# Counts of repeated edges made by VectorE and written by plain scatters, in groups of eight behind each chunk's sixteen gathers

## The chip, the cores and the metric

The kernel runs on one core of one Trainium2 chip. The metric is device time in microseconds (us) of that core; lower is better. The engines are named as in the profile: PE (TensorE), DVE (VectorE), ACT (ScalarE), POOL (GpSimd), SP (SyncE).

## What is computed

Four graph layers run one after another over the same 6250 nodes of 128 features and the same 106250 edges, which are sorted by receiver. Each layer is added to its input and normalised:

```python
edge_index = jnp.stack([src, dst])
x = _layernorm(x + _L0_gnn_ref(x, edge_index, ...))                  # attention, both directions
x = _layernorm(x + _L1_gnn_ref(x, ..., src, dst, edge_type_4))       # two attention layers, 4 relations
x = _layernorm(x + _L2_gnn_ref(x, edge_index, ...))                  # graph convolution
x = _layernorm(x + _L3_gnn_ref(x, edge_index, edge_weight1, ...))    # sum over edges, then a two-layer network
```

The part that the change touches is a matrix that the last two layers use. Their sums over edges are of this kind:

```python
msgs = h[src] * norm[:, None]
agg = jax.ops.segment_sum(msgs, dst, num_segments=n) + b
```

The kernel computes them as a dense product with a matrix `adj` of edge counts: the entry for receiver r and sender s is how many edges run between them, 0 for most, 1 for most of the rest, 2 or more where an edge is repeated.

## The kernel before

The edges lie as 128 partitions of `EC` = 832 columns, in the order of the receiver. The stages run one after the other, with a barrier between them: sorting and counting (`place_edges` twice, called plc1 and plc0; plc0 also makes the tables by edge, in steps called `table_part`, one per group of 8 columns), two sweeps of the first layer, a turn layer t0, the attention sweep of the second layer's first half (below: first sweep), turn layer t1, the second attention sweep (second sweep), turn layer t2, and the dense layers.

An attention sweep goes over the 832 columns in `NCK` = 52 chunks of `CK` = 16. For each chunk POOL issues 16 indirect gathers of one column each (128 rows of 256 words out of the node table, tile `l_swp_G`, L1465), into a ring of `GR` = 4 chunks. DVE makes the 16 query rows (`query`, L1580), multiplies and reduces them (`multiply`, `reduce`), and does the running maximum, the weighting and the long scan of the softmax (L1605 to L1645); ACT turns values, exponentiates and makes the result rows; SP loads queries and stores rows. POOL may start the gathers of chunk c when DVE's `weigh` of chunk c - 4 has told `used`. DVE handles chunk c's front part while it makes the queries of chunk c + 1, and waits in `multiply` for the gathers of chunk c + 1. When the last row is stored, POOL gathers the rows of first segments (`l_swp_FR`), DVE and PE merge the ends of partitions, and POOL scatters them back.

`adj` has 2-byte entries and is cleared early. It is filled by 832 indirect DMAs, one per column of edges, each of which adds the constant 1 into 128 cells (`CELL` holds the numbers of the cells). Two adds into one cell must not be in flight together, so `put_cell` (L1410) has POOL wait, before each add, until the one before has landed:

```python
pool.wait_ge(g.landed, 16 * g.put)
pool.indirect_dma_start(out=g.cells, ..., in_=g.ONE[:, 0:1], in_offset=None, compute_op=ALU.add)
```

These adds stand in POOL's program between other work: 49 in turn layer t0 (one behind each scatter of queries, `put_query`, L1807), then in the first sweep one behind every second gather (`EVERY` = 2, so 8 per chunk), with 8 and 3 more at its end, 49 in t1, and the rest in the second sweep, where the last of them starts at 7761.3 us and the last chunks have gathers alone. In the turn layers PE, DVE and ACT make a query row for each of 49 groups of nodes; `t_qr` is a ring of four of them, emptied by `put_query`.

## Time and profile before

| | |
|---|---|
| median of 3 runs | 9291.03 us (9284.9 to 9291.43) |
| the profiled execution | 9288.31 us, span 9286.2 us |
| busy over the span | POOL 62%, DVE 54%, ACT 31%, PE 30% |
| first sweep, first gather to end of last | 3849.7 to 5899.1 us |
| second sweep, the same | 6244.3 to 8035.5 us |
| turn layers | t0 3504 to 3850 us, t1 5949 to 6244 us, t2 8078 to 8254 us |

The profiled execution is 2.7 us under the median and within the range of the runs. Busy shares are means over stages with different limits; the stage is what counts. Indirect DMAs are listed on POOL by the time in which POOL writes their descriptors; the transfer itself follows.

### The profile page before, as it was taken

What the parts mean: (1) busy time and instruction counts of PE and PEld (TensorE: products, weight loads), DVE (VectorE), ACT (ScalarE), POOL (GpSimd) and SP (SyncE); (2) the same over time, 40 slices, a digit from 0 to 9 for tenths busy, and PEclk for the clock granted to TensorE, in tenths of its full rate; (3) what the DMA queues carried; (4) which work ended last, traced back from release to release, by engine and by line L of the source; (5) the groups of instructions that cost most, each with busy time, mean ns of one, the idle gap of its engine ahead of it and who ended that gap; (6) DMA issues with size and microseconds to landing.
All of it is one profiled execution on the core that took longest, in us unless ns stands there. A gap on an engine that the chain in (4) does not pass through costs nothing. (4 is left out here: it accounts for less than half of the span.)

```text
span 9286.2 us, 65164 instructions
## 1 busy us (share of the span) xinstructions
PE 2819.9 (30%) x19883; PEld 2216.5 (24%) x19883; DVE 4982.0 (54%) x8546; ACT 2921.4 (31%) x3159; POOL 5776.8 (62%) x5419
## 2 busy tenths in 40 slices
PE   5666635555100005400000000270000000059997
PEld 5666525555100005300000000160000000034443
DVE  7555547766699996444444444434444446740212
ACT  6333313333366662222222222232222223410001
POOL 2777777777777767677777777657777777610000
PEclk8555555555555557755555555585555555569998
DMA  5655224444466655444444434453444445546653
GB/s 140 212 197 191 82 72 143 130 135 133 152 217 217 219 198 155 134 109 111 111 110 111 110 103 111 112 156 98 110 111 111 111 111 159 182 72 192 196 189 115
DMA packets 576000, 1306.03 MB, mean 141 GB/s; under 512 B 249724, under 2 KB 344654, under 8 KB 521766
## 3 DMA queue, kind: packets, MB, share of 16 engines
q1 hardware_dynamic: 252742, 889.07, 28.3%
q0 software_dynamic: 292960, 358.27, 16.7%
q10 hardware_dynamic: 29952, 54.54, 2.4%
q8 instruction: 161, 2.64, 0.1%
q14 instruction: 185, 1.52, 0.1%
HBM read 782.92 MB, written 518.52 MB: 140 GB/s over the span
## 5 line engine op out<-in xcount | busy, mean ns | idle before, releaser
L1465 POOL DMA_INDIRECT l_swp_G<-table,KVI x1664 | 1605.2, 965 | 512.5 <-issue 327.1
L1410 POOL DMA_INDIRECT adj<-ONE,CELL x832 | 1344.2, 1616 | 728.0 <-DMA adj<-ONE,CELL 486.7
L1586 DVE TENSOR_TENSOR l_swp_PROD<-l_swp_G,l_swp_QS 128x1024 f32<-128x1024 f32 x208 | 253.9, 1221 | 2005.5 <-DMA l_swp_G<-table,KVI 2005.4
L1691 PE MATMUL l_swp_AW<-l_swp_ET,ones 128*128 128x512 f32 x4 | 4.2, 1141 | 3932.3 <-DVE l_swp_ET L1669 3932.3
L1110 POOL DMA_INDIRECT arrived<-plc_QS,plc_idx x832 | 814.1, 979 | 253.6 <-issue 245.4
L1110 POOL DMA_INDIRECT slots<-REC,plc_idx x832 | 796.9, 958 | 273.4 <-issue 252.8
L1522 ACT ACTIVATE l_swp_VT<-l_swp_G 128x2048 f32<-128x2048 f32 x104 | 385.8, 3710 | 1826.6 <-issue 1692.4
L1195 POOL DMA_INDIRECT l_G<-table,OTHI x832 | 786.2, 945 | 256.1 <-issue 252.9
L1691 PEld LDWEIGHTS l_swp_AW<-l_swp_ET,ones 128*128 128x128 f32 x4 | 1.0, 312 | 3932.6 <-DVE l_swp_ET L1669 3932.6
L949 PE MATMUL plc_pr<-plc_seen,plc_otf 128*128 128x49 f32 x3328 | 861.6, 414 | 12.8 <-DVE plc_seen L698 12.8
L949 PEld LDWEIGHTS plc_pr<-plc_seen,plc_otf 128*128 128x128 f32 x3328 | 846.8, 326 | 32.4 <-issue 32.1
L1580 DVE SCALAR_TENSOR_TENSOR l_swp_QS<-l_swp_QS,KEEP,l_swp_QX 128x128 f32<-128x128 f32 x1664 | 586.6, 353 | 44.3 <-DMA l_swp_QX<-queries 6.7
L1332 DVE TENSOR_TENSOR_SCAN l_X<-l_AW,l_X 128x2244 f32<-128x2244 f32 x104 | 502.5, 4831 | 3.6
L1639 DVE TENSOR_TENSOR_SCAN l_swp_X<-l_swp_AW,l_swp_X 128x2244 f32<-128x2244 f32 x104 | 501.0, 4818 | 0.1
L1063 ACT ACTIVATE plc_otb<-plc_otf 128x1024 bf16<-128x1024 f32 x208 | 219.9, 1057 | 778.7 <-PE plc_pe_q L938 775.1
L759 DVE SCALAR_TENSOR_TENSOR plc_QS<-plc_QS,KEEP,plc_QX 128x136 f32<-128x136 f32 x831 | 288.4, 347 | 316.2 <-DMA arrived<-plc_QS,plc_idx 173.1
L951 PEld LDWEIGHTS plc_pr<-plc_ohi,plc_bm 128*128 128x128 bf16 x1664 | 445.2, 268 | 0.0
L2448 PE MATMUL dn_acc<-dn_AR,HP 128*128 128x512 f16 (+1 forms) x1950 | 424.4, 375 | 33.8 <-DMA dn_AR<-adj 30.9
L2448 PE MATMUL dn_acc<-dn_AR,dn_HP 128*128 128x512 f16 (+1 forms) x1950 | 419.8, 372 | 4.8 <-ACT dn_HP L2657 2.0
L1263 ACT ACTIVATE l_ROW<-l_X 128x2112 f32<-128x2112 f32 x104 | 407.5, 3918 | 2.2 <-DVE l_X L1332 2.2
L1543 ACT ACTIVATE l_swp_ROW<-l_swp_X 128x2112 f32<-128x2112 f32 x104 | 407.5, 3918 | 0.0
L951 PE MATMUL plc_pr<-plc_ohi,plc_bm 128*128 128x49 bf16 x1664 | 394.3, 237 | 0.0
(502 smaller groups left out, 8294.6 us busy)
## 6 DMA issues: line engine op xcount, KB each, us to landing
sums<-l_ROW SPq DMA_DIRECT2D x104, 1088.0 KB, 4.7
l_swp_QX<-queries SPq DMA_DIRECT2D x104, 1088.0 KB, 7.8
dn_AR<-adj SPq DMA_DIRECT2D x100, 832.0 KB, 4.6
adj<-plc_zrow SPq DMA_DIRECT2D x100, 800.0 KB
dn_AR<-adj SPq DMA_DIRECT2D x100, 768.0 KB, 4.3
queries<-plc_zrow SPq DMA_DIRECT2D x55, 1088.0 KB
sums<-l_swp_ROW SPq DMA_DIRECT2D x52, 1096.0 KB, 5.5
plc_QX<-queries SPq DMA_DIRECT2D x104, 544.0 KB, 4.4
```

Source lines behind the costliest of these rows:

```text
L949: pe.matmul(pr[:, b, j * NB:(j + 1) * NB], otf[:, c % FB, j, :], seen[:, b, :, j], start=True, stop=False)
L951: last = pe.matmul(pr[:, b, j * NB:(j + 1) * NB], bm[:, b, j, :], column(ohi[:, c % HB, :, :, :], j), start=False, stop=True)
L1110: pool.indirect_dma_start(out=slots, out_offset=bass.IndirectOffsetOnAxis(ap=idx[:, c % IB, j:j + 1], axis=0), in_=g.REC[:, c * CH + j, :] ...
L1195: pool.indirect_dma_start(out=G[:, p % GR, j, :], out_offset=None, in_=table, in_offset=bass.IndirectOffsetOnAxis(ap=g.OTHI[:, x:x + 1], a ...
L1263: act.activation(ROW[:, c % 2, :, 0:D + H], X[:, c % 2, :, :, 1:CK + 1].rearrange("p h d c -> p c (h d)"), ACT.Copy).then_inc(rowed, 1)
L1332: v.tensor_tensor_scan(X[:, b, :, :, :].rearrange("p h d c -> p (h d c)"), AF[:, :, :, :].rearrange("p h d c -> p (h d c)"), X[:, b, :, :, ...
L1410: pool.indirect_dma_start(out=g.cells, out_offset=bass.IndirectOffsetOnAxis(ap=g.CELL[:, g.put:g.put + 1], axis=0), in_=g.ONE[:, 0:1], in_ ...
L1465: pool.indirect_dma_start(out=G[:, c % GR, j, :], out_offset=None, in_=table, in_offset=bass.IndirectOffsetOnAxis(ap=index[:, c * CK + j:c ...
L1543: act.activation(ROW[:, c % 2, :, 0:D + H], X[:, c % 2, :, :, 1:CK + 1].rearrange("p h d c -> p c (h d)"), ACT.Copy).then_inc(rowed, 1)
L1580: v.scalar_tensor_tensor(out=QS[:, j, :], in0=QS[:, j - 1 if j else QH - 1, :], scalar=g.KEEP[:, n:n + 1], in1=QX[:, c % QB, x, 0:D], op0= ...
L1639: v.tensor_tensor_scan(X[:, b, :, :, :].rearrange("p h d c -> p (h d c)"), AF[:, :, :, :].rearrange("p h d c -> p (h d c)"), X[:, b, :, :, ...
L2448: last = pe.matmul(acc[m][:, 0:z], HP[:, j, part, :], AR[:, i % RING_A, (q - first) * P:(q - first) * P + z], start=(j == 0 and part == 0) ...
```

## The change

The adds become plain scatters. In plc0, `table_part` gets eight more steps (i from 11 to 18): a key per edge (`KEY`: receiver times 8192 plus sender, as f32) and a mark (`AGAIN`) on an edge whose key stands earlier in its group of 8 columns. In the two attention sweeps DVE takes 8 columns of edges per chunk. For each of the eight, `later` compares the key with all keys to the right of it in its partition and counts the equal ones with the instruction's accumulator. Then `cells` looks with `max_index` for an equal key to the left, adds 1 to the counts (`VAL`), and points the cell of every edge that is not the first of its kind to a spare cell. So the first edge of a kind writes the whole count, and nothing is added in memory. The eight scatters of a chunk stand behind its 16 gathers, `BEHIND` = 5 chunks after DVE has handled them; they wait for `celled`, never for a landing. The turn layer t0 has no scatters into `adj` any more, t1 has 16, each sweep has 16 + 8 at its end, and t2 has 16 behind its fetches, before the dense layers read `adj`.

```diff
-EVERY = 2
+BEHIND = 5
...
+                elif i == 11:
+                    link(v.tensor_tensor_scan(t[:, :], F[:, :], F[:, :], 0.0, ALU.add, ALU.max))
+                    link(v.scalar_tensor_tensor(out=g.KEY[:, :], in0=t[:, :], scalar=float(1 << SHIFT), in1=g.OTHI[:, :],
+                                                op0=ALU.mult, op1=ALU.add))
+                    link(v.memset(g.AGAIN[:, :, :], 0.0))
+                    v.tensor_scalar(g.SPARE[:, :], g.minus[:, :], float(-(1 << SHIFT)), float((NB + 1) * P), ALU.mult, ALU.add)
+                elif i < 19:
+                    d = i - 11
+                    key = g.KEY[:, :].rearrange("p (q i) -> p q i", i=8)
+                    same = t[:, 0:EC // 8 * (8 - d)].rearrange("p (q i) -> p q i", i=8 - d)
+                    link(v.tensor_tensor(same, key[:, :, d:8], key[:, :, 0:8 - d], ALU.is_equal))
+                    link(v.tensor_tensor(g.AGAIN[:, :, d:8], g.AGAIN[:, :, d:8], same, ALU.max))
...
-def put_cell(pool, passed, g):
-
-
-    if g.put < EC:
-        if g.put:
-            pool.wait_ge(g.landed, 16 * g.put)
+def put_cell(pool, passed, g, upto):
+
+
+    if g.put < upto * 8:
+        if g.put % 8 == 0:
+            pool.wait_ge(g.celled, g.put // 8 + 1)
             passed()
         pool.indirect_dma_start(out=g.cells, out_offset=bass.IndirectOffsetOnAxis(ap=g.CELL[:, g.put:g.put + 1], axis=0),
-                                in_=g.ONE[:, 0:1], in_offset=None, compute_op=ALU.add).then_inc(g.landed, 16)
+                                in_=g.VAL[:, g.put:g.put + 1], in_offset=None).then_inc(g.landed, 16)
         g.put += 1
...
-                    if j % EVERY == EVERY - 1:
-                        put_cell(pool, passed, g)
-            for _ in range(8):
-                put_cell(pool, passed, g)
+                if c >= BEHIND:
+                    for _ in range(8):
+                        put_cell(pool, passed, g, (part + 1) * NCK)
+            for _ in range(16):
+                put_cell(pool, passed, g, (part + 1) * NCK)
...
-            for _ in range(3):
-                put_cell(pool, passed, g)
+            for _ in range(8):
+                put_cell(pool, passed, g, (part + 1) * NCK)
...
+            def later(c, i):
+                q = part * NCK + c
+                x = q * 8 + i
+                if i >= 2:
+                    v.wait_ge(told, pick.n + i - 1)
+                if x == EC - 1:
+                    v.memset(RPT[:, i:i + 1], 0.0).then_inc(told, 1)
+                else:
+                    v.tensor_scalar(EQ[:, x % 2, 0:EC - 1 - x], g.KEY[:, x + 1:EC], g.KEY[:, x:x + 1], 0.0, ALU.is_equal, ALU.add,
+                                    accum_out=RPT[:, i:i + 1]).then_inc(told, 1)
+
+            def cells(c):
+                q = part * NCK + c
+                at = slice(q * 8, q * 8 + 8)
+                v.max_index(FIND[:, :], g.KEY[:, at], g.KEY[:, 0:q * 8 + 8]).then_inc(told, 1)
+                pick.n += 9
+                v.wait_ge(told, pick.n)
+                v.tensor_scalar(g.VAL[:, at], RPT[:, :], 1.0, None, ALU.add)
+                pick(v.scalar_tensor_tensor(out=DROP[:, 0, :], in0=FIND[:, :], scalar=float(-q * 8), in1=g.iota[:, 0:8],
+                                            op0=ALU.add, op1=ALU.not_equal))
+                v.tensor_tensor(DROP[:, 1, :], DROP[:, 0, :], g.AGAIN[:, q, :], ALU.max)
+                pick(v.tensor_scalar(AWAY[:, :], g.iota[:, 0:8], g.SPARE[:, 0:1], float(q * 8), ALU.add, ALU.add))
+                pick(v.copy_predicated(g.CELL[:, at], DROP[:, 1, :], AWAY[:, :]))
+                v.sem_inc(g.celled, 1)
...
+                    if c >= 0 and x % 2 == 1:
+                        later(c, x // 2)
...
+                if c >= 0:
+                    cells(c)
```

On POOL, in the first sweep, one chunk reads before like this (`l_swp_G` are the gathers, `adj` the adds), eight times over:

```order
L1465 DMA l_swp_G<-table,KVI 128x256 x2
L1410 DMA adj<-ONE,CELL 52428800x1
L1465 DMA l_swp_G<-table,KVI 128x256 x2
L1410 DMA adj<-ONE,CELL 52428800x1
L1465 DMA l_swp_G<-table,KVI 128x256 x2
```

And the same engine at the start of that sweep after the change:

```order
L1484 DMA l_swp_G<-table,KVI 128x256 x96
L1422 DMA adj<-VAL,CELL 52428800x1 x8
L1484 DMA l_swp_G<-table,KVI 128x256 x16
L1422 DMA adj<-VAL,CELL 52428800x1 x8
L1484 DMA l_swp_G<-table,KVI 128x256 x16
```

The first six chunks of gathers have nothing between them, and from then on 8 scatters stand behind each 16 gathers.

On DVE, in the first sweep, the middle of a chunk after the change (chunk 1; `l_swp_QS` are the query rows, `l_swp_EQ,l_swp_RPT<-KEY` are `later`'s compares):

```order
L1651 TENSOR_TENSOR l_swp_X<-l_swp_VT,l_swp_AW 128x4x32x16
L1676 TENSOR_SCALAR l_swp_EQ,l_swp_RPT<-KEY 128x821
L1601 SCALAR_TENSOR_TENSOR l_swp_QS<-l_swp_QS,KEEP,l_swp_QX 128x128
L1660 SCALAR_TENSOR_TENSOR l_swp_X<-l_swp_AW,l_swp_X 128x2244
L1601 SCALAR_TENSOR_TENSOR l_swp_QS<-l_swp_QS,KEEP,l_swp_QX 128x128
L1666 COPY l_swp_X<-l_swp_X 128x132
L1676 TENSOR_SCALAR l_swp_EQ,l_swp_RPT<-KEY 128x820
L1607 TENSOR_TENSOR l_swp_PROD<-l_swp_G,l_swp_QS 128x1024
```

Two of the chunk's eight compares are seen here, inside the chain that ends in `used` and in the next chunk's products; before the change the same rows stand without them. At the chunk's end come the six instructions of `cells`:

```order
L1611 TENSOR_REDUCE l_swp_LB<-l_swp_PROD 128x8x4 x2
L1682 MAX_INDEX l_swp_FIND<-KEY 128x8
L1685 TENSOR_SCALAR VAL<-l_swp_RPT 128x8
L1686 SCALAR_TENSOR_TENSOR l_swp_DROP<-l_swp_FIND,iota 128x8
L1688 TENSOR_TENSOR l_swp_DROP<-l_swp_DROP,AGAIN 128x8
L1689 TENSOR_SCALAR l_swp_AWAY<-iota,SPARE 128x8
L1690 COPY_PREDICATED CELL<-l_swp_DROP,l_swp_AWAY 128x8
```

The compare's length shrinks by one with each column, from 831 elements in the first chunk of the first sweep to 416 at its end, and from 415 to 0 in the second sweep; the length that `max_index` looks through grows by 8 a chunk, from 8 to 832.

## Rows read from the trace of the kernel before

**Rows 1.** The page, busy time, share and instructions of each engine
```profile
PE 2819.9 (30%) x19883; PEld 2216.5 (24%) x19883; DVE 4982.0 (54%) x8546; ACT 2921.4 (31%) x3159; POOL 5776.8 (62%) x5419
```

**Rows 2.** Busy us of each engine in two stretches, the two sweeps
```profile
3849.70:5899.10 2049.40, 0.00 (x0) 0.00 (x0) 898.83 (x1445) 520.66 (x357) 1474.81 (x1247) 0.50 0.41 109
6244.30:8035.50 1791.20, 0.00 (x0) 0.00 (x0) 893.50 (x1441) 522.01 (x406) 1296.37 (x1139) 0.50 0.44 124
```

**Rows 3.** POOL's groups by line, first sweep (busy, mean | idle before, releaser)
```profile
L1465 POOL DMA_INDIRECT l_swp_G<-table,KVI x832 | 805.3, 968 | 256.3 <-issue 151.0 <-DMA adj<-ONE,CELL 105.4
L1410 POOL DMA_INDIRECT adj<-ONE,CELL x415 | 669.5, 1613 | 321.4 <-DMA adj<-ONE,CELL 199.9 <-issue 121.5
```

**Rows 4.** POOL's groups by line, second sweep
```profile
L1465 POOL DMA_INDIRECT l_swp_G<-table,KVI x832 | 799.9, 961 | 256.1 <-issue 176.1 <-DMA adj<-ONE,CELL 77.1 <-POOLq L93 2.9
L1410 POOL DMA_INDIRECT adj<-ONE,CELL x307 | 496.5, 1617 | 241.6 <-DMA adj<-ONE,CELL 154.2 <-issue 87.4
```

**Rows 5.** POOL's timeline, first sweep (start, us, operation, idle before)
```profile
4311.40 1.61 POOL L1410 DMA_INDIRECT adj<-ONE,CELL  x1 [4.18 <-DMA adj<-ONE,CELL]
```

**Rows 6.** Adds into adj, issue to landing
```profile
DMA to landing us min/median/max: 2.9/3.1/9.1
```

**Rows 7.** POOL's groups by line where no adds are left
```profile
L1465 POOL DMA_INDIRECT l_swp_G<-table,KVI x161 | 152.2, 946 | 49.0 <-issue 49.0
```

**Rows 8.** POOL's groups by line, whole span
```profile
L1110 POOL DMA_INDIRECT arrived<-plc_QS,plc_idx x832 | 814.1, 979 | 253.6 <-issue 245.4 <-DVE plc_idx L721 7.9 <-DMA arrived<-plc_QS,plc_idx 0.3
L1827 POOL DMA_INDIRECT adj<-ONE,ODD x1 | 1.0, 984 | 0.3 <-issue 0.3
```

**Rows 9.** DVE's timeline, second sweep, no adds left
```profile
7917.26 1.22 DVE L1586 TENSOR_TENSOR l_swp_PROD<-l_swp_G,l_swp_QS 128x1024 f32<-128x1024 f32 x1 [2.28 <-DMA l_swp_G<-table,KVI]
7937.27 1.22 DVE L1586 TENSOR_TENSOR l_swp_PROD<-l_swp_G,l_swp_QS 128x1024 f32<-128x1024 f32 x1 [2.26 <-DMA l_swp_G<-table,KVI]
```

**Rows 10.** DVE's groups by form, whole span
```profile
L844 DVE TENSOR_SCALAR plc_tab_t<-plc_tab_F 128x832 f32<-128x832 f32 x1 | 0.6, 595 | 0.0
L438 DVE TENSOR_REDUCE plc_tab_small<-plc_tab_t 128x1 f32<-128x832 f32 x2 | 2.0, 1020 | 0.1
L851 DVE TENSOR_TENSOR_SCAN shared<-plc_tab_t,plc_tab_rec 128x832 f32<-128x832 f32 x4 | 7.6, 1894 | 0.0
L721 DVE TENSOR_SCALAR plc_idx<-plc_pos 128x8 uint32<-128x8 f32 x208 | 40.8, 196 | 447.7 <-DMA slots<-REC,plc_idx 445.3
```

**Rows 11.** Timeline of a turn layer, DVE and POOL side by side
```profile
3547.50 1.08 DVE L1988 TENSOR_TENSOR HH<-HH,t_par 128x896 f32<-128x896 f32 x1
3547.59 1.80 POOL L1792 DMA_INDIRECT t_NV<-sums,LASTI  x1 [0.30 <-issue]
```

**Rows 12.** POOL's timeline, ends of the two sweeps
```profile
5945.74 0.99 POOL L1481 DMA_INDIRECT sums<-l_swp_FR,BACKI  x1 [0.30 <-issue]
...
8065.02 0.95 POOL L1475 DMA_INDIRECT l_swp_FR<-sums,FIRSTI  x1 [29.52 <-DMA sums<-l_swp_ROW]
8074.64 0.98 POOL L1481 DMA_INDIRECT sums<-l_swp_FR,BACKI  x1 [8.67 <-DVE l_swp_FR L1686]
```

**Rows 13.** POOL's timeline, first and last of the query scatters in two turn layers
```profile
3577.99 0.98 POOL L1807 DMA_INDIRECT queries<-t_qr,STARTI  x1 [0.30 <-issue]
...
3841.89 0.99 POOL L1841 DMA_INDIRECT t_first<-queries,SEGI  x1 [0.30 <-issue]
...
6013.38 1.00 POOL L1807 DMA_INDIRECT queries<-t_qr,STARTI  x1 [0.30 <-issue]
...
6236.93 0.99 POOL L1841 DMA_INDIRECT t_first<-queries,SEGI  x1 [0.31 <-issue]
```

**Rows 14.** ACT's timeline, two query rows in succession
```profile
6104.37 0.27 ACT L2162 ACTIVATE t_qr<-t_pq 128x128 f32<-128x128 f32 x1
...
6108.42 0.27 ACT L2162 ACTIVATE t_qr<-t_pq 128x128 f32<-128x128 f32 x1
```

**Rows 15.** Waits in 1410 to 1560 us: total us, times, longest
```profile
DVE plc_QS L759 <- DMA arrived<-plc_QS,plc_idx: 29.1, 11, 4.2
```

More of the change, by code:

```diff
@@ L916, in _ @@
                     reached(n)
-                    if 0 <= c - 1 < 11:
+                    if 0 <= c - 1 < 19:
                         table_part(c - 1)
@@ L1400, in _ @@
                 o.then_inc(added, 1)
-def put_cell(pool, passed, g):
-    if g.put < EC:
-        if g.put:
-            pool.wait_ge(g.landed, 16 * g.put)
+def put_cell(pool, passed, g, upto):
+    if g.put < upto * 8:
+        if g.put % 8 == 0:
+            pool.wait_ge(g.celled, g.put // 8 + 1)
             passed()
         pool.indirect_dma_start(out=g.cells, out_offset=bass.IndirectOffsetOnAxis(ap=g.CELL[:, g.put:g.put + 1], axis=0),
-                                in_=g.ONE[:, 0:1], in_offset=None, compute_op=ALU.add).then_inc(g.landed, 16)
+                                in_=g.VAL[:, g.put:g.put + 1], in_offset=None).then_inc(g.landed, 16)
         g.put += 1
 def attention_sweep(nc, g, k, table, width, index, voff, array, out, weights, tag):
+    part = 1 if weights else 0
     ro = RO + 1 if weights else RO
@@ L1430, in attention_sweep @@
         weighed = s.sem("weighed")
+        told = s.sem("told")
+        RPT = s.sb("RPT", [P, 8])
+        EQ = s.sb("EQ", [P, 2, EC], BF16)
+        FIND = s.sb("FIND", [P, 8], U32)
+        DROP = s.sb("DROP", [P, 2, 8], U32)
+        AWAY = s.sb("AWAY", [P, 8], U32)
         init = s.sem("init")
@@ L1561, in _ @@
             link = Chain(v, chain)
+            pick = Chain(v, told)
             v.memset(FL[:, :, :, 0:1], -BIG)
@@ L1816, in _ @@
                         put_query(n - AHEAD * GT + 1)
-                        put_cell(pool, passed, g)
                 for n in range(NB - AHEAD * GT + 1, NB):
                     put_query(n)
-                    put_cell(pool, passed, g)
             else:
@@ L1823, in _ @@
                     fetch(n)
-                    if gcn and n % 3 == 2:
-                        put_cell(pool, passed, g)
                 if gcn:
@@ L1829, in _ @@
                     for _ in range(EC):
-                        put_cell(pool, passed, g)
+                        put_cell(pool, passed, g, 2 * NCK)
                     pool.wait_ge(lone, 16)
@@ L1835, in _ @@
                         put_query(n)
-                        put_cell(pool, passed, g)
+                        put_cell(pool, passed, g, NCK)
             if not gcn:
@@ L2782, in gnn_kernel @@
         g.ONE = sb("ONE", [P, 1], F16)
+        g.KEY = sb("KEY", [P, EC])
+        g.VAL = sb("VAL", [P, EC], F16)
+        g.AGAIN = sb("AGAIN", [P, EC // 8, 8], BF16)
+        g.SPARE = sb("SPARE", [P, 1])
+        g.celled = nc.alloc_semaphore("celled", num=max(nc.free_semaphores))
         g.landed = nc.alloc_semaphore("landed", num=max(nc.free_semaphores))
```

## The prediction

> **What bounds the kernel now.** I read the busy shares first: POOL 62%, DVE 54% [rows 1]. No engine is near full, so the stages have to be looked at one by one. In the two attention sweeps (2049.4 and 1791.2 us, 41% of the span together) DVE is busy 899 and 894 us, ACT 521 and 522, PE not at all, POOL 1475 and 1296 [rows 2]. The groups of POOL by line close the account: in the first sweep the gathers take 805.3 busy + 256.3 idle = 1061.6 us and the adds 669.5 + 321.4 = 990.9, together 2052.5 of 2049.4 [rows 3]; in the second 1056.0 + 738.1 = 1794.1 of 1791.2 [rows 4]. So POOL's program in order is the length of a sweep, and half of it is the adds: 2.39 us for each (990.9 / 415), of which 1.61 is the writing of descriptors and the rest waits. The reader is to see one such wait in the timeline: POOL stands 4.18 us before an add, released by the landing of the one before [rows 5]; adds land 2.9 to 9.1 us after their issue, 3.1 in the median [rows 6].
>
> **The sweeps, POOL.** Once the adds have run out, a gather costs (152.2 + 49.0) / 161 = 1.250 us [rows 7], so 832 cost 1040 us. The price of a plain scatter: the nearest row in kind is the one into `adj` of a single column with 2-byte data, 0.984 + 0.3 us; the nearest in number are the 832 scatters of plc0, issued eight in a row, (814.1 + 253.6) / 832 = 1.283 us [rows 8]. They agree, and I take 1.283. Bounds: 1.250, as a gather; above, no row of these reaches the add's 1.92. From first to last gather of a sweep stand 46 groups of eight (behind chunks 5 to 50): 368 x 1.283 = 472 us. A sweep is then 1512 us: 2049.4 - 1512 = 538 less in the first, 1791.2 - 1512 = 279 less in the second. The second gains less since its last 14 chunks have no adds now.
>
> **The sweeps, DVE.** This holds only while DVE needs less than POOL's 16 x 1.250 + 8 x 1.283 = 30.3 us for a chunk. Without adds the same DVE work repeats every 7937.27 - 7917.26 = 20.01 us with 2.26 idle: 17.75 us [rows 9]. New are eight compares and `cells`. The trace has no compare with an accumulator and no `max_index`. From below: a plain TENSOR_SCALAR over 832 f32 takes 0.595 us; from above: a scan, which carries a value from element to element, 1.894; between them a reduction, which like the compare reads one f32 tensor and gives one value, 1.020; one over 8 elements takes 0.196 [rows 10]. I take the reduction as nearest in kind: 0.19 + 0.0010 n us. The mean length in the first sweep is 623: 0.81 x 8 = 6.5 us; `cells` is one look through 212 elements in the mean, 0.4, and five small ones at 0.2, 1.4 together. DVE: 17.75 + 6.5 + 1.4 = 25.7 us a chunk, 27.2 in the first chunks. In the second sweep the mean length is 207: 17.75 + 3.2 + 1.8 = 22.8. Both lie under 30.3, so DVE's addition costs nothing; the cover is 4.6 us a chunk in the first sweep, and beyond it each us costs 52. The first five chunks are gathers alone, 20.0 us each, and DVE at 27.2 falls behind. POOL is held only if `weigh` of chunk c - 4 is late: for chunk 5, wanted at 100 us, it comes at about 25 + 2 x 27.2 + 8 = 87 us. From there POOL is the slower one. `celled` is told some four chunks before its scatters.
>
> **The shared resource.** In a turn layer an indirect DMA on POOL takes 1.80 us instead of 0.95 while DVE runs a TENSOR_TENSOR on two SBUF tensors of 896 elements [rows 11]. The sweep's long DVE instructions do not show this: gathers there stay at 0.946 us [rows 7]. Of the new ones three a chunk read two SBUF tensors or more, over 8 elements, 0.2 us each. If each met POOL, 3 x 0.2 x 104 = 62 us; I take 10. The Trainium skill, page "SBUF — State Buffer", section "Who interferes with whom", says that `tensor_scalar` in a two-port mode locks GpSimd out of a shared port pair, but not in the form that writes out its accumulator. By that rule the eight compares cost POOL nothing; if the exception did not hold here, the sum would be that of the second rival. No row of before shows the accumulating form.
>
> **Ends of the sweeps.** From the end of the last gather to the end of the scatter back it is 5946.7 - 5899.1 = 47.6 us in the first and 8075.6 - 8035.5 = 40.1 in the second, where no adds stand and the rows are ready 29.5 us after the last gather [rows 2, 12]. After: 24 scatters are 30.8 us, then the gather of first rows 1.25, eight scatters 10.3 (DVE's merge of 8.7 lies under them), 1.3 for the scatter back: 43.6 in each. DVE's last chunk has up to 4 us more, mostly under ACT's rows. Sum 4 less, 3.5 more: 0.
>
> **Turn layers.** t0 from its first query scatter to the gather that follows the last takes 263.9 us, t1 223.6, each with 49 adds among 49 queries [rows 13]. Without adds the other engines set the pace: two successive query rows are 4.05 us apart where nothing is waited for [rows 14]. Four rows are ready at the start, so the floor is 45 x 4.05 + 5 = 187 us. t1 keeps 16 scatters, 1.3 + 1.3 us with the query beside them, under 4.05. Other waits (normalisation once per seven groups, transfers) stay: between floor and now I take 4.8 us a row in t0, which has more of them, and 4.25 in t1: 220 and 195 us, 44 and 28 less. Ends: floor in both (77 and 37 less), or nothing.
>
> **What I cost at nothing.** plc0's new steps: the first is one scan (1.9), one pass (1.1), a memset and a small one, about 3.6 us; the other seven are two passes over 416 elements in the mean, about 1.2 us. In that stretch DVE waits 29.1 us of 150 for landings of POOL's scatters alone, about 2 us in a chunk of 10 [rows 15]; uncovered it would be 12 us. The 16 scatters in t2 end at about 8170 us by today's clock, the layer at 8254.
>
> **Sum.** 538 + 279 + 44 + 28 - 10 = 879 us less, on the profiled execution's own 9288.3: 8409. The median of the runs stands 2.7 above that execution: 8412 us.
>
> **Rivals.**
> *DVE becomes the bound of the first sweep.* For it: the price of the compare is not in the trace. At the scan's 2.28 ns per element, chunk 0 needs 17.75 + 15.1 + 1.2 = 34 us, falling by 0.13 a chunk to 30.3 at chunk 29; the mean excess of 1.9 over 29 chunks is 54, with the longer look about 60: 8472 us. It decides from (30.3 - 17.75 - 1.4) / 8 = 1.39 us per compare. Against: the scan is slow because it feeds itself; a reduction does not. In the second sweep even that price leaves DVE under POOL.
> *The compares hold POOL up.* For it: the 1.80 us [rows 11]. If POOL stood still for all of every compare, 52 x 6.5 + 52 x 3.2 = 504 us, for half of it 250: 8660 to 8910 us. Against: the compare reads one tensor, not two.
> *The small scatters clog their queue (slower than before).* If a scatter of 128 cells of 2 bytes held the next DMA for as long as an add takes to land, 3.1 us [rows 6], the 800 of the two sweeps would cost 1.82 more each, 1456 us: 9868. It decides from 1.283 + 879 / 800 = 2.38 us each. For it: before, never were two of them in flight. Against: plc0 issues eight scatters in a row at 1.283 us and is not held [rows 8], and the DMA engines are busy 0.41 of the first sweep only [rows 2]. The Trainium skill, page "DMA: Bandwidth & Descriptors", section "Specifications", says that below 512 bytes the DMA reads, modifies and writes. That speaks for a dear write; no run so far shows whether it holds a queue.
>
> **Chances.** Forecast 0.73; DVE bound 0.12; POOL held up 0.08; queue clogged 0.05; something else 0.02. Differences within 0.2% (19 us) can't be told from no change. Faster 0.94, same 0.01, slower 0.05. Low end: scatters as gathers (24 less), turn layers at the floor (42 less), no meeting on the port (10): 8336, so 8340. High end: the DVE rival at 8472 with the short instructions always meeting POOL (52): 8524, so 8530. That holds the forecast and the first rival, and leaves out the others.
>
> **What would show it.** `adj` scatters at 0.98 us with 0.3 idle and no wait on a landing; a chunk of 30.3 us on POOL; both sweeps about 1512 us; DVE waiting for gathers in each chunk after the first ten; compares at 0.8 us in the first sweep. Wrong if POOL waits on `used` (DVE), if gathers or scatters are longer than 1.0 us where compares run, or if POOL idles before a scatter.

## The result, and the profile after

The changed kernel takes 8362.7 us (median of 4 runs, 8358.0 to 8374.7) against 9288.2 us for the kernel before, measured beside it; the ratio is 0.9006 (95% interval 0.899 to 0.9021). The forecast was 8412 us, 49 us too much. The profiled run took 8357.96 us.

The page of the changed kernel, busy time, share and instructions of each engine:

```profile
PE 2793.5 (33%) x19883; PEld 2195.0 (26%) x19883; DVE 5570.0 (67%) x10955; ACT 2920.7 (35%) x3159; POOL 5222.9 (63%) x5419
```

POOL has the same 5419 instructions as before [rows 1] and 554 us less to do. DVE has 588 us more, and is now the busiest engine by the share. Which of the two sets the end can't be read from this line. The busy us of each engine in the two sweeps, first to last gather (as [rows 2]; the last three numbers are PE's granted clock, the DMA share, GB/s):

```profile
3789.40:5299.00 1509.60, 0.00 (x0) 0.00 (x0) 1253.32 (x2604) 519.99 (x357) 1144.22 (x1200) 0.50 0.46 147
5602.90:7113.60 1510.70, 0.00 (x0) 0.00 (x0) 1103.29 (x2605) 524.48 (x406) 1145.33 (x1200) 0.50 0.46 148
```

POOL's two groups by line in the first sweep, as [rows 3] (busy us, mean ns | idle us before them, and its releaser), and its timeline where a chunk's eight scatters meet the gathers of the next:

```profile
L1484 POOL DMA_INDIRECT l_swp_G<-table,KVI x832 | 789.3, 949 | 256.0 <-issue 253.2 <-POOLq L93 2.8
L1422 POOL DMA_INDIRECT adj<-VAL,CELL x368 | 354.9, 965 | 112.2 <-issue 112.2
```

```profile
4119.60 0.95 POOL L1484 DMA_INDIRECT l_swp_G<-table,KVI  x1 [0.30 <-issue]
4120.85 1.00 POOL L1422 DMA_INDIRECT adj<-VAL,CELL  x1 [0.30 <-issue]
4122.15 0.97 POOL L1422 DMA_INDIRECT adj<-VAL,CELL  x1 [0.30 <-issue]
...
4129.75 0.96 POOL L1422 DMA_INDIRECT adj<-VAL,CELL  x1 [0.30 <-issue]
4131.01 0.98 POOL L1484 DMA_INDIRECT l_swp_G<-table,KVI  x1 [0.30 <-issue]
```

789.3 + 256.0 + 354.9 + 112.2 = 1512.4, of which 2.8 lie ahead of the first gather, so 1509.6, the whole sweep: POOL goes from instruction to instruction with 0.30 us between them and waits for nobody. A gather costs 1.256 us and a scatter (354.9 + 112.2) / 368 = 1.269. The waits for a landing that filled [rows 3 to 5] are gone. The engine that waits is now DVE. Its new work in the first sweep by line, and what it waits for in the first and in the second sweep (us in total, times, longest):

```profile
L1676 DVE TENSOR_SCALAR_CACHE_REDUCE l_swp_EQ<-KEY 128x831 bf16<-128x831 f32 (+57 forms) x406 | 348.3, 858 | 0.0
L1676 DVE DVE_READ_ACCUMULATOR l_swp_EQ<-KEY 128x1 f32 x406 | 33.2, 82 | 0.0
L1682 DVE FIND_INDEX8 l_swp_FIND<-KEY 128x8 uint32<-128x8 f32 (+49 forms) x50 | 18.2, 364 | 0.0
```

```profile
DVE l_swp_PROD L1607 <- DMA l_swp_G<-table,KVI: 220.4, 51, 8.2
DVE l_swp_PROD L1607 <- DMA l_swp_G<-table,KVI: 373.7, 68, 10.5
```

DVE needs (1509.6 - 220.4) / 52 = 24.8 us a chunk in the first sweep and (1510.7 - 373.7) / 52 = 21.9 in the second, and stands for the rest until POOL's gathers have landed.

The turn layers come next. POOL's timeline, first query scatter and the gather behind the last, of t0 and of t1, as [rows 13]:

```profile
3578.33 0.99 POOL L1857 DMA_INDIRECT queries<-t_qr,STARTI  x1 [0.30 <-issue]
...
3782.22 0.98 POOL L1887 DMA_INDIRECT t_first<-queries,SEGI  x1 [3.60 <-DMA queries<-t_qr,STARTI]
...
5409.97 0.98 POOL L1857 DMA_INDIRECT queries<-t_qr,STARTI  x1 [0.30 <-issue]
...
5595.80 0.98 POOL L1887 DMA_INDIRECT t_first<-queries,SEGI  x1 [3.03 <-DMA queries<-t_qr,STARTI]
```

They take 203.9 and 185.8 us where it was 263.9 and 223.6, and in t0 POOL now waits for ACT's query rows:

```profile
POOL queries L1857 <- ACT t_qr L2208: 71.3, 25, 4.1
```

The account closes: 2049.4 - 1509.6 = 539.8 and 1791.2 - 1510.7 = 280.5 from the sweeps, 60.0 and 37.8 from the turn layers, 1 from the ends, 10.8 from the last turn layer and the dense layer together, less 0.3 ahead of t0, where the changed kernel is the later one: 929.6 us, and the two profiled runs lie 9288.3 - 8358.0 = 930.3 apart. The remaining 0.7 us lies in the short gaps between these stretches.

### The profile page after: what moved, and what is told of

It reads as the page before. It is cut to its first block and busy times, and to the rows that moved or that the text cites. A ratio compares the mean times of both kernels' runs of the same rounds, so it can differ in the third digit from the quotient of the medians.

```text
span 8356.2 us, 66957 instructions
## 1 busy us (share of the span) xinstructions
PE 2793.5 (33%) x19883; PEld 2195.0 (26%) x19883; DVE 5570.0 (67%) x10955; ACT 2920.7 (35%) x3159; POOL 5222.9 (63%) x5419
## 5 line engine op out<-in xcount | busy, mean ns | idle before, releaser
L1484 POOL DMA_INDIRECT l_swp_G<-table,KVI x1664 | 1579.0, 949 | 511.9 <-issue 506.3
L1422 POOL DMA_INDIRECT adj<-VAL,CELL x832 | 809.9, 973 | 253.7 <-issue 253.1
L1676 DVE TENSOR_SCALAR_CACHE_REDUCE l_swp_EQ<-KEY 128x831 bf16<-128x831 f32 (+63 forms) x831 | 528.6, 637 | 0.0
L1548 ACT ACTIVATE l_swp_AW<-l_swp_DW 128x64 f32<-128x64 f32 x104 | 23.7, 228 | 1359.5 <-DVE l_swp_X L1666 1345.2
L2494 PE MATMUL dn_acc<-dn_AR,HP 128*128 128x512 f16 (+1 forms) x1950 | 425.4, 375 | 27.8 <-DMA dn_AR<-adj 24.8
```

Source lines behind the costliest of these rows:

```text
L1422: pool.indirect_dma_start(out=g.cells, out_offset=bass.IndirectOffsetOnAxis(ap=g.CELL[:, g.put:g.put + 1], axis=0), in_=g.VAL[:, g.put:g.p ...
L1484: pool.indirect_dma_start(out=G[:, c % GR, j, :], out_offset=None, in_=table, in_offset=bass.IndirectOffsetOnAxis(ap=index[:, c * CK + j:c ...
L1676: v.tensor_scalar(EQ[:, x % 2, 0:EC - 1 - x], g.KEY[:, x + 1:EC], g.KEY[:, x:x + 1], 0.0, ALU.is_equal, ALU.add, accum_out=RPT[:, i:i + 1] ...
L2494: last = pe.matmul(acc[m][:, 0:z], HP[:, j, part, :], AR[:, i % RING_A, (q - first) * P:(q - first) * P + z], start=(j == 0 and part == 0) ...
```

## The experiments

**Theory A:** the length of a sweep is POOL's program in order; an add was dear by its descriptors (1.61 us against 0.97) and by the wait for the landing before it; DVE's new work lies under POOL. **Rivals:** the waits alone were the cost; accumulating writes hold their queue; the compares cost POOL something, or DVE is the bound already.

**1. The price of the descriptors.** All 832 writes add into cleared, now distinct cells, and nothing waits for a landing.

```
-                                in_=g.VAL[:, g.put:g.put + 1], in_offset=None).then_inc(g.landed, 16)
+                                in_=g.VAL[:, g.put:g.put + 1], in_offset=None, compute_op=ALU.add).then_inc(g.landed, 16)
```

> The changed kernel, but each of its 832 scatters is an accumulating one (it adds VAL to the cleared cell), with no wait for a landing. Theory A (POOL's account in order: an add costs the 1.61 us in which its descriptors are written plus 0.3, a plain scatter 0.97 + 0.31): 368 adds between the first and last gather of each sweep by 0.64 us more, 235 us; 24 at each end, 15 us; together +500 us, 8860 us, sweeps about 1745 us long. Rival B (the descriptors cost nothing extra; only the waits for landings made the adds dear): 8363 us. Rival C (accumulating writes hold their queue until they have landed, wait or no wait): 3.1 us each instead of 1.28, +1500 us, 9870 us.

Measured: 8843.8 us (ratio 0.9511, 0.9495 to 0.9526). The group of the adds over the whole span in this kernel:

```profile
L1422 POOL DMA_INDIRECT adj<-VAL,CELL x832 | 1300.0, 1563 | 253.6 <-issue 253.3 <-DVE l_swp_FR L1736 0.3
```

Sweeps of 1732.2 and 1733.8 us: 222.6 and 223.1 more than the changed kernel, 0.605 us for each of 368. The idle time is that of plain scatters, so nearly all of it is the instruction itself, 1563 ns against 973 in the mean of 832. The forecast of 8860 us was 16 too high, since it took 0.64 us for this difference. Both rivals fall: the descriptors have a price without any wait, and a queue of adds is not held.

**2. The place alone.** One plain scatter behind every second gather instead of eight behind sixteen.

```
-                if c >= BEHIND:
-                    for _ in range(8):
-                        put_cell(pool, passed, g, (part + 1) * NCK)
+                    if c >= BEHIND and j % 2 == 1:
+                        put_cell(pool, passed, g, (part + 1) * NCK)
```

> The changed kernel, but one plain scatter stands behind every second gather (from the sixth chunk on) instead of eight behind sixteen, no wait for a landing: position alone. Theory A (only the sum of POOL's instructions counts): 8363 us, sweeps 1510 us. Rival (a small write among the gathers holds the gather behind it, or the reverse): above 8400 us. Second rival (eight in a row back up in the queue, which the changed kernel pays and this one does not): under 8340 us.

Measured: 8396.6 us (0.9033, 0.9018 to 0.9048). Neither 8363 nor above 8400: sweeps of 1530.1 and 1530.8 us, 20 more each. POOL's groups in the first of them:

```profile
L1484 POOL DMA_INDIRECT l_swp_G<-table,KVI x832 | 793.1, 953 | 256.3 <-issue 252.2 <-POOLq L93 2.8 <-DVE l_swp_X L1650 1.2
L1422 POOL DMA_INDIRECT adj<-VAL,CELL x375 | 369.2, 985 | 114.3 <-issue 114.3
```

Between the first and the last gather stand 375 scatters here and not 368, because seven of the last chunk's eight now come before its last gather. These seven, 9 of the 20 us, are moved from behind the sweep and not added. The other 11 us are longer instructions: scatters of 985 ns instead of 965, gathers of 953 instead of 949. That is (369.2 / 375 - 0.965) + (793.1 - 789.3) / 375 = 0.030 us per scatter for standing among gathers. Standing together is worth about 23 us in the whole kernel (POOL's gathers and scatters are busy 2388.9 us in the changed kernel, 2411.7 here), a small part of the change that I had put at nothing.

**3. The wait alone.** The same, with the wait for the landing of the scatter before, which is the order of the kernel before.

```
+        if g.put:
+            pool.wait_ge(g.landed, 16 * g.put)
```

> As e_apart, and each plain scatter waits until the one before it has landed: the order and the waits of the kernel before, with plain scatters in place of adds. Theory A: a landing of 2.6 to 2.9 us after issue stands against two gathers of 1.25 between two scatters, so 0.3 to 0.7 us of wait each; 368 in each sweep, 110 to 260 us a sweep, +220 to +520 us, 8580 to 8890 us. With e_accum it should divide the 2.39 us of an add of before: 1.28 plain, 0.64 descriptors, the rest wait. Rival B (the waits are all of the cost): as before without the turn layers' gain, about 9150 us. Rival D (a plain scatter lands so fast that the wait is hidden under two gathers): 8363 us.

Measured: 8826.8 us (0.9497, 0.9482 to 0.9513). Sweeps of 1685.5 and 1724.6 us, 155.4 and 193.8 over experiment 2: 0.466 us for each of 750 scatters, in the range of theory A, but not for the reason given. I had expected a little from every scatter. In the trace seven of eight wait for nothing, and one in a chunk (94 of the 750) stands idle for more than 1 us, 4.0 in the mean. The kernel before is the same: 86 of the 722 adds in its sweeps stand idle for 4.0 to 5.0 us, as the one of [rows 5], and nearly all others for the 0.3 us of the issue. What POOL waited for at its scatters (whole span: us, times), and its timeline (scatters only) beside SP's queue:

```profile
  DMA adj<-VAL,CELL: 510.4, 156
```

```profile
4520.69 0.99 POOL L1424 DMA_INDIRECT adj<-VAL,CELL  x1 [0.30 <-issue]
...
4524.49 0.98 POOL L1424 DMA_INDIRECT adj<-VAL,CELL  x1 [0.30 <-issue]
...
4530.94 0.98 POOL L1424 DMA_INDIRECT adj<-VAL,CELL  x1 [2.94 <-DMA adj<-VAL,CELL]
...
4534.74 0.98 POOL L1424 DMA_INDIRECT adj<-VAL,CELL  x1 [0.30 <-issue]
```

```profile
4521.41 0.32 SPq L1523 DMA_DIRECT2D sums<-l_swp_ROW  x1
4521.77 0.43 SPq L1514 DMA_DIRECT2D l_swp_QX<-queries  x1
```

The late landing is that of the scatter issued at 4524.5, right behind the chunk's two transfers of 1088 KB; the same pair stands at 4554.5, and the scatter after it waits 2.99 us at 4564.1. The rest of the trace agrees. Of the 750 scatters 93 land more than 4.5 us after their issue, and all 93 were issued between 0.6 us before and 2.8 us after such a transfer; the other 657 land within 3.8 us, and 3 of them were issued in that interval. In the kernel before 86 of 722 adds land later than 4.5 us, all issued 0.1 to 3.0 us after such a transfer. In experiment 4, where the scatters stand elsewhere in the chunk, 4 of 736 do. So the late landings go with the large transfers; that the transfers are their cause is likely, but no run took them away.

**4. The wait where the scatters stand together.** The changed kernel with the wait of experiment 3.

> The changed kernel with its eight scatters behind sixteen gathers, but each waits for the landing of the one before it. Theory A: with nothing between two scatters the whole way to the landing is open: about 0.97 + 2.8 + 0.2 = 4.0 us each instead of 1.28 for 7 of 8 in each chunk, and 0 to 1 us for the first; 46 chunks in two sweeps by 19 us, +1750 us, about 10200 us with the ends: slower than the kernel before. So the place behind the gathers is only to be had without the wait. Rival D (a landing is quick when the queue is empty, under 1.3 us): 8400 us.

Measured: 9549.4 us (1.0273, 1.0252 to 1.0293), slower than the kernel before, though every write is plain. POOL's timeline:

```profile
4214.04 1.00 POOL L1424 DMA_INDIRECT adj<-VAL,CELL  x1 [0.30 <-issue]
4217.01 0.97 POOL L1424 DMA_INDIRECT adj<-VAL,CELL  x1 [1.97 <-DMA adj<-VAL,CELL]
4219.94 0.96 POOL L1424 DMA_INDIRECT adj<-VAL,CELL  x1 [1.96 <-DMA adj<-VAL,CELL]
```

The sign was right, the size not: a scatter starts 2.9 us after the one before it, not 4.0. From issue to landing the trace gives 2.1 us for these, in the median, where I had taken the 2.8 of the gathers and added the instruction and 0.2 to it. Grouping the scatters and dropping the wait belong together: the first without the second costs more than the whole change gains.

**5. Less work for DVE.** Every compare looks at the 64 edges behind its own only, which gives the same counts on these inputs.

```
-                    v.tensor_scalar(EQ[:, x % 2, 0:EC - 1 - x], g.KEY[:, x + 1:EC], ...
+                    n = min(64, EC - 1 - x)
+                    v.tensor_scalar(EQ[:, x % 2, 0:n], g.KEY[:, x + 1:x + 1 + n], ...
```

> The changed kernel with every compare cut to the 64 edges behind its own (on these inputs the same counts come out, since the edges of a receiver stand together). DVE has about 5 us less to do in a chunk of the first sweep, 1.7 in the second. Theory A (DVE's new work lies under POOL): 8363 us, nothing won, and DVE's waits for gathers grow by some 260 and 90 us. Rival (the compares hold POOL up or DVE is the bound in the first chunks): 8300 us or less, with fewer or shorter POOL instructions in the first sweep.

Measured: 8367.8 us (0.9005), beside 8367.7 (0.9002) for the changed kernel. DVE lost 235 us of work in the first sweep and 63 in the second and waited 236 and 63 us longer for gathers; POOL's busy time stood still, and so did the sweeps:

```profile
3792.30:5301.80 1509.50, 0.00 (x0) 0.00 (x0) 1017.87 (x2604) 520.36 (x357) 1144.12 (x1200) 0.50 0.46 148
5606.70:7117.20 1510.50, 0.00 (x0) 0.00 (x0) 1039.91 (x2605) 524.47 (x406) 1145.16 (x1200) 0.50 0.46 148
```

This is the cleanest evidence that the length of the compares costs nothing, neither as DVE's time nor as a hindrance to POOL.

**6. More work for DVE.** Every compare twice, the second into tiles that nobody reads.

```
+                    v.tensor_scalar(EQ2[:, x % 2, 0:EC - 1 - x], g.KEY[:, x + 1:EC], g.KEY[:, x:x + 1], 0.0, ALU.is_equal, ALU.add,
+                                    accum_out=RPT2[:, i:i + 1])
```

> The changed kernel with every compare made twice, the second into tiles of its own that nobody reads. With a compare at 0.235 + 0.0010 n us and 0.08 for the reading of its accumulator, a chunk c of the first sweep costs DVE about 35.4 - 0.12 c us, over POOL's 30.3 until chunk 42; in the second it stays under 28. Theory A (threshold where DVE passes POOL's 30.3): first sweep 25 + 43 x 32.9 + 6 x 30.3 = 1620 to 1650 us, POOL waiting for DVE's `used`; second sweep 1510; 8475 to 8510 us. Rival (compares hold POOL up in proportion): both sweeps longer, the second by at least half as much as the first. Rival (DVE has still room): 8363 us.

Measured: 8475.0 us (0.9119, 0.9104 to 0.9134), the low end of the expectation, but by two errors that cancel. What POOL waited for in the first sweep, and the two sweeps:

```profile
POOL l_swp_G L1486 <- DVE l_swp_X L1653: 71.2, 29, 4.2
```

```profile
3791.80:5366.20 1574.40, 0.00 (x0) 0.00 (x0) 1527.40 (x3326) 498.78 (x345) 1144.22 (x1200) 0.50 0.42 140
5716.00:7226.60 1510.60, 0.00 (x0) 0.00 (x0) 1246.30 (x3417) 523.46 (x406) 1145.30 (x1200) 0.50 0.46 148
```

DVE is busy 97% of the first sweep and POOL waits for its `used`. The second sweep has 143 us more of the same compares and is not a microsecond longer, which speaks against any hold on POOL. The errors: the first sweep's gathers end 65 us later, not 110 or more, and the other 45 us stand behind them, since DVE is up to four chunks back when POOL has finished (from the last gather to the scatter back it is now 5454.3 - 5366.2 = 88 us instead of 43).

**7. No scatters in the sweeps.** The scatters in the sweeps and at their ends are taken out: one stands behind each query row of t1, all others in the last turn layer.

> The changed kernel with no scatter in the sweeps: 98 go beside the 98... queries of the second turn layer, one behind each, and the other 734 in the last turn layer in a row. POOL needs 20 us a chunk, so DVE sets the sweeps' pace. Theory A: 26.3 - 0.056 c us a chunk in the first sweep and 23.4 - 0.056 c in the second, 1245 and 1105 us from first to last gather (265 and 405 less); the second turn layer unchanged at 186 us; the last turn layer longer by 734 x 1.28 less the 103 us in which POOL stood idle or scattered there, about 840: 8530 us in all. Rival (scatters in a row clog their queue): more than 1.4 us a scatter in the last turn layer, 8620 us or more.

Measured: 8701.1 us (0.9361, 0.9345 to 0.9376). The two sweeps:

```profile
3793.50:5049.90 1256.40, 0.00 (x0) 0.00 (x0) 1209.69 (x2531) 499.17 (x345) 786.45 (x832) 0.50 0.52 176
5394.10:6507.70 1113.60, 0.00 (x0) 0.00 (x0) 1065.29 (x2537) 502.13 (x392) 787.28 (x832) 0.50 0.59 198
```

1256 and 1114 us for 1245 and 1105: DVE's limit is close to where the sum of its instructions puts it, 253 and 397 us under the changed kernel. The total missed by 171 us, 20 of them in the sweeps. A turn layer has 49 query rows, not the 98 of the expectation, so 783 scatters fell to the last one and not 734 (63 us); the ends of the sweeps are 38 and 30 us longer, as in experiment 6, which I had left out; and in the last turn layer a scatter took (767.5 + 254.9) / 783 = 1.306 us. In a row without any gather between them, 783 small scatters do not clog their queue.

**8. The turn layers.** The kernel before without its 98 adds in t0 and t1.

> The kernel before, adds and all, but with no add in the two turn layers: those 98 move into the second sweep. Theory A (the adds alone made the turn layers longer; the rest of them waits for the query rows): t0 and t1 as in the changed kernel, 204 and 186 us from the first query scatter to the gather behind the last, 60 and 38 less than before; first sweep 2050; second sweep 1791 + 98 x 2.39 = 2025 us; 9290 - 98 + 234 = 9426 us. Rival (something else than the adds' own time made them long): 264 and 224 us stay, 9525 us.

On the chip on which this and the next two kernels ran, the kernel before took 10107.8 us and not 9290. In the traces of these three the instructions have their usual durations, but DVE and ACT stand before single ones, up to 26 us in the placing stage. Only what ran on this chip is compared here. Measured: 10225.1 us, ratio 1.0118 (1.0097 to 1.0139), a little under the forecast of 9426 / 9290 = 1.0146 and far from the rival's 1.0253. t0 took 4527.2 - 4294.2 = 233.0 us and t1 199.7; the next kernel, with plain scatters, took 236.9 and 199.9 on the same chip. So a turn layer without adds is as long as one of a kernel with plain scatters, whatever the kind of write elsewhere, and 49 scatters behind the rows of t1 cost it nothing. What t0 and t1 of the kernel before take on this chip isn't known.

**9. Scatters moved to where POOL is idle.** 49 scatters of the first sweep go behind the query rows of t1 (16 in the changed kernel), 76 of the second into the last turn layer (16 in the changed kernel). A second kernel has two scatters behind each of these rows, 98, and 288 between the gathers of the first sweep.

```
+SHARES = (337, 310)
...
-                if c >= BEHIND:
-                    for _ in range(8):
+                if BEHIND <= c < NCK - 1:
+                    share, d = (SHARES[part], c - BEHIND)
+                    for _ in range(share * (d + 1) // 46 - share * d // 46):
                         put_cell(pool, passed, g, (part + 1) * NCK)
-            for _ in range(16):
+            for _ in range(22):
```

> The changed kernel with the same 832 scatters, shifted from POOL's full stretches to its idle ones: the first sweep leaves 49 to the second turn layer (one behind each query row, where the changed kernel has 16), the second sweep leaves 76 to the last turn layer (changed kernel: 16), where POOL stood idle 82 us before the adjacency matrix was read. 337 and 310 instead of 368 stand between first and last gather, 22 instead of 16 behind it. Theory A: sweeps 1040 + 337 x 1.283 = 1472 and 1438 us, 38 and 72 less; ends 2.5 less each; turn layers unchanged; 8367 - 115 = 8252 us. Rival (the dense layer waits for the last scatter now): 8300 us or more, the dense layer starting later than 200 us after the last turn layer began. Rival (DVE is the bound at this rate): POOL waits for `used`, 8290 us or more.

> As e_one, with two scatters behind each query row of the second turn layer (98 there, 288 in the first sweep). POOL needs 3 x 1.28 = 3.85 us for a row that comes every 3.8 us in the mean. Theory A: first sweep 1040 + 288 x 1.283 = 1410 us, 100 less; second 1438, 72 less; ends 5 less; second turn layer 10 longer (about 192 to 196 us from first to last query scatter... where 182 now); 8367 - 167 = 8200 us. Rival (POOL becomes the bound of the turn layer and the gain of moving them is lost): as e_one, 8250 us. Rival (DVE bound at 27 us a chunk): POOL waits for `used` in the first chunks, 8230 us or more.

Measured on the chip with the 10108: 9682.1 us (0.9586, 0.9562 to 0.9609) and 9690.4 (0.9604, 0.9574 to 0.9634). There, by the releasers, DVE was the bound of both sweeps (POOL waited 543 us for `used`), so these two runs do not test the forecasts. They do say that the second scatter behind each row of t1 is no gift: t1 took 6645.0 - 6392.0 = 253.0 us instead of 199.9, for 46.6 us less in the first sweep. The first of the two was run once more, on another chip:

> The kernel of e_one again, unchanged, since in that call the kernel before itself took 10108 us instead of 9290 (DVE and ACT stood before single instructions there, in every stage, at unchanged durations of the instructions). Theory A where the kernel before takes 9290: sweeps 1472 and 1438 us, ends 41 each, turn layers unchanged, 8252 us, ratio 0.888. Rival (the dense layer waits for the last scatter): 8300 us or more. Rival (DVE is the bound at this rate even there): POOL waits for `used`, 8290 us or more. Where the kernel before takes 10108 again: 9680 us, ratio 0.958.

Measured: 8255.8 us, with the kernel before at 9293.5; ratio 0.8887 (0.8875 to 0.8899), against 0.9002 (0.8987 to 0.9017) of the changed kernel. The sweeps of this kernel:

```profile
3787.20:5257.60 1470.40, 0.00 (x0) 0.00 (x0) 1252.71 (x2604) 519.84 (x357) 1114.46 (x1169) 0.50 0.47 151
5560.80:6998.10 1437.30, 0.00 (x0) 0.00 (x0) 1103.99 (x2605) 524.26 (x406) 1089.71 (x1142) 0.50 0.48 155
```

1470 and 1437 us for a forecast of 1472 and 1438; t1 185.8 as in the changed kernel; the whole kernel 4 us from the forecast. It is faster than both. The last scatter is issued 182 us after the last turn layer begins, and the first load of the adjacency matrix 9 us later, at 192 where the changed kernel has 181: that room is now used up.

**10. The changed kernel once more.** It is unchanged.

> The changed kernel itself once more, as the measure for the runs of this call and for the spread of its stages. Theory: 8363 us, sweeps 1510 us each to within 2 us; the 10.9 us less in the last two stages (t2 and the dense layer) that the first profiled run showed come back or not; if they are spread, that stretch lies between 1197 and 1208 us.

Measured: 8367.7 us. The sweeps are 1509.9 and 1510.6 us, within 0.3 of the first profile. The stretch from the last turn layer to the end is 1211.0 us, over the 1197 to 1208 that I gave. The rows of the last turn layer and the dense layer in the kernel before, in the changed one, and in this run of it:

```profile
8078.55:9286.20 1207.65, 1004.53 (x4743) 509.09 (x4743) 304.16 (x568) 140.48 (x244) 60.38 (x53) 0.88 0.52 154
```

```profile
7159.38:8356.20 1196.82, 1004.95 (x4743) 508.96 (x4743) 304.55 (x568) 140.48 (x244) 81.72 (x69) 0.89 0.53 156
```

```profile
7160.13:8371.10 1210.97, 1000.72 (x4743) 507.94 (x4743) 304.79 (x568) 140.53 (x244) 80.91 (x69) 0.88 0.53 154
```

The same kernel gives 1196.8 and 1211.0, so the 10.8 us that this stretch seemed to give is spread of the run. Most of the difference (11.8 of 14.2 us) is between the issue of the first load of the adjacency matrix and PE's first matmul on it: 7340.1 to 7363.7 in one, 7343.9 to 7379.3 in the other.

## Why the prediction was right, step by step

**POOL's program is the length of a sweep.** Right: 1509.6 and 1510.7 us for 1512 in both. Experiments 5 and 9 show it from two sides, less work for DVE for no time, fewer instructions on POOL for just their sum.

**An add is 2.39 us, a scatter 1.283.** Right, and the difference can now be divided. Per write: 1.27 plain, 0.605 for the descriptors of an add (experiment 1), 0.466 for the wait (experiment 3 against 2), 0.030 for the place (experiment 2). Together 2.37, against 2.39 in [rows 3]. Of the change's 820 us in the sweeps that gives, for the 722 adds there, about 440 to the plain descriptors, 340 to the dropped wait and 20 to the place; the remaining 20 are not divided. An add's instruction took 1.61 us among gathers and takes 1.56 in experiment 1, where the adds stand together. The wait can be read from the kernel before as well: an instruction of POOL has 0.305 us before it in any case, and beyond that the adds stood idle (321.4 - 126.6) / 415 = 0.469 us [rows 3] and (241.6 - 93.6) / 307 = 0.482 [rows 4]. So of the 0.78 us that the prediction called waits 0.305 were none, and the rest came from one add in eight.

**DVE 25.7 and 22.8 us a chunk.** Measured are 24.8 and 21.9 (the sweep less the waits for gathers), and 24.2 and 21.4 in experiment 7, where DVE sets the pace. The compare takes 0.858 us in the mean of the first sweep and the reading of its accumulator 0.082, together 0.94 for a forecast of 0.81. Eight of them are 7.5 us and not 6.5, and yet the chunk was 0.9 shorter than forecast. The timeline shows why:

```profile
4132.09 0.95 DVE L1676 TENSOR_SCALAR_CACHE_REDUCE l_swp_EQ<-KEY 128x735 bf16<-128x735 f32 x1
4132.97 0.08 DVE L1676 DVE_READ_ACCUMULATOR l_swp_EQ<-KEY 128x1 f32 x1
4132.97 0.35 DVE L1601 SCALAR_TENSOR_TENSOR l_swp_QS<-l_swp_QS,KEEP,l_swp_QX 128x128 f32<-128x128 f32 x1
```

The compare lasts until 4133.04, but the reading and the instruction after it both start at 4132.97: one instruction's duration reaches into the next. So durations added up are too much. The new groups sum to 452 us in the first sweep (8.7 a chunk), while DVE's busy time grew by 1253.3 - 898.8 = 354 (6.8 a chunk). A dear compare and this overlap are two errors of opposite sign, of which the second is the larger. In the first chunks DVE was as near to its limit as forecast, 146.5 us busy in 150, and POOL never waited.

**The port, 10 us.** Nothing is seen of it. Gathers are 949 ns in both sweeps, 946 before [rows 7], and 945 and 946 in experiment 7, with the compares and without scatters, so the 3 ns are not the compares'. By the Trainium skill's page "SBUF — State Buffer", section "Who interferes with whom", the form of `tensor_scalar` that writes out its accumulator does not lock GpSimd out; the trace agrees, with 143 us more of such compares in the second sweep of experiment 6 at 1510.6 us.

**Turn layers 44 and 28 us.** The mechanism was right, the size too small: 60 and 38. I had taken 4.8 us a row in t0 and 4.25 in t1, a middle between the floor and the time with adds, for other waits. t1 took 185.8, which is the floor of 187. t0 took 203.9, by the forecast's own formula (203.9 - 5) / 45 = 4.42 us a row. So the other waits are not there in t1, and in t0 they are half of what I took. This is the largest error of the sum, 26 of about 50 us.

**The rest.** The ends of the sweeps changed by 1 us (forecast 0), the placing stage by 0.3 (forecast 0). 11 us are the spread shown in experiment 10, 3 the sweeps (the first one's 2049.4 - 1512 is 537 and not the 538 of the sum), 10 the port. That the total came within 49 us is no luck of errors that cancel: all of these have the same sign.

**The rivals.** "DVE becomes the bound": false with one compare of 0.94 us, true with two of them (experiment 6), so the threshold of 1.39 lies between as it should; the runs do not place it closer. "The compares hold POOL up": false, experiments 5 and 6. "The small scatters clog their queue": false, by the 1.269 us of a scatter in the changed kernel and by experiments 1 and 7. The Trainium skill's page "DMA: Bandwidth & Descriptors", section "Specifications", has the DMA read, modify and write for less than 512 bytes; if these 2-byte writes pay for that, it shows nowhere in the issue, which goes on every 1.27 us.

## What to carry to other kernels

Where one engine's program in order is the length of a stage, price the stage as count times period for each kind of instruction, and read the period as busy plus idle over the count. That sum met the sweeps of the changed kernel and of experiments 1, 5 and 9 within 1%, and experiment 2 within 1.4%, nearly half of which is the seven scatters that I had not counted. It says at once what moving an instruction to another stage is worth. Work moved from such an engine to one that waits is free up to a threshold, and the threshold is to be worked out before: here 30.3 us a chunk. Beyond it the loss comes at the end of the stage as well, since the engine that is behind has several chunks left when the other has finished. A chain of "wait until the last one has landed" costs little while other instructions stand between its members, and a great deal once they are put together: 0.47 us a scatter against (2053.9 - 1509.6) / 368 = 1.48 in experiment 4.

## What the runs showed of the hardware

An indirect scatter of 128 cells of 2 bytes takes POOL 0.97 us, the same with an accumulating write 1.56, in a run without any wait. Standing one by one among the gathers costs 0.03 us per scatter. A scatter lands 2.1 to 2.2 us after its issue in the median, and 4.7 to 8.2 us after it where two transfers of 1088 KB are issued at about the same time (experiment 3). The compare with an accumulator shows as two instructions, 0.858 us for 623 f32 elements and 0.082 for the reading. On one chip the kernel before took 8.8% longer. The three kernels profiled there have instructions of the usual durations and stalls of up to 26 us before single ones. DVE's waits in the first kernel of experiment 9 name a releaser, `remote`, that no profile from another chip has (us in total, times, longest):

```profile
DVE plc_hits L708 <- remote: 607.3, 84, 21.0
DVE shared L735 <- remote: 511.6, 45, 20.6
DVE l_swp_QS L1603 <- remote: 391.8, 160, 4.0
```

What these stalls wait for stays open, and so does whether they belong to the chip or to the time of these runs, since no later run was on that chip. They fall on DVE and ACT, and none of POOL's waits has this releaser, so a kernel in which DVE lies just under POOL loses much of its gain there: the version of experiment 9 has a ratio of 0.9586 there and of 0.8887 elsewhere.
